# A two-layer kernel on one core: the quantised branch of the mixing layer is laid out by channels from tile 8 on

## The reference, cut to what matters

```
xn = layernorm(x)
x  = x + ssm_block(xn) + quantised_linear(xn)

quantised_linear(xn):
    for every token and every block of 32 channels:
        scale = max(max|xn| / 7.5, 1e-30)
        q     = xn / scale, each rounded to the nearest number of the FP6 (E2M3) grid
    out = (q * scale) @ wd.T + bias          # wd: the weight, quantised in the same way
```

## Time and profile before

| what | value |
|---|---|
| time, median of 3 runs | 2079.48 us (2079.25 to 2079.97) |
| time of the profiled execution | 2080.59 us |
| its span, first to last instruction | 2078.8 us |
| PE busy | 2063.7 us (99%) |
| DVE busy | 1523.1 us (73%) |
| ACT busy | 1095.0 us (53%) |
| POOL busy | 840.9 us (40%) |
| granted clock of PE | 0.999 of full speed |
| read from HBM, written to HBM | 160.88 MB, 100.79 MB |

### The profile page before, as it was taken

The page is one execution under the profiler, slowest core; times in us unless marked ns, Lnnn a source line. Parts: engine busy times, 40 slices in busy tenths (PEclk is TensorE's granted clock), DMA queues, the critical chain, the costliest instruction groups (busy, mean ns, idle before and its releaser), DMA issues.

```text
span 2078.8 us, 27463 instructions
## 1 busy us (share of the span) xinstructions
PE 2063.7 (99%) x9263; PEld 1645.9 (79%) x9263; DVE 1523.1 (73%) x2973; ACT 1095.0 (53%) x1842; POOL 840.9 (40%) x842
## 2 busy tenths in 40 slices
PE   9999999999999999999999999999999999999998
PEld 7887888444688888888888888788888888888887
DVE  6998775666787777776777875677777676677776
ACT  4555556223455555555555555755555555555553
POOL 1011110455545454554444453144444444444444
PEclk9999999999999999999999999999999999999999
DMA  5666662976533333333333332422222222222211
GB/s 199 251 220 226 202 210 103 292 254 208 176 122 102 108 116 103 131 102 102 122 119 105 115 119 101 152 71 72 71 72 74 90 91 86 88 71 72 71 41 41
DMA packets 179750, 263.47 MB, mean 127 GB/s; under 512 B 20377, under 2 KB 110745, under 8 KB 177050
## 3 DMA queue, kind: packets, MB, share of 16 engines
q1 hardware_dynamic: 166488, 238.18, 34.7%
q10 hardware_dynamic: 13122, 23.53, 3.1%
HBM read 160.88 MB, written 100.79 MB: 126 GB/s over the span
## 4 chain that ended last, share of the span: by engine, by line
PE 89%; DVE 5%; ACT 2%; issue 2%; POOL 1%; DMA 1%; SPq 0%; POOLq 0%; ACTq 0%
PE bank L102 23%; PE bank L104 23%; PE bank L103 23%; PE bank L1512 7%; PE bank L2068 3%; PE bank L901 3%; PE bank L922 3%; PE bank L919 3%; PE bank L1468 2%; PE bank L645 1%; DVE e_w_lo L1895 0%; DVE d_x L1364 0%; DVE d_xq L1335 0%; DVE d_stats L1366 0%; PE bank L1526 0%
## 5 line engine op out<-in xcount | busy, mean ns | idle before, releaser
L102 PE MATMUL bank<-e_ring,e_w_hi 128*128 128x512 f32 x512 | 200.8, 392 | 0.0
L103 PE MATMUL bank<-e_ring,e_w_hi 128*128 128x512 f32 x512 | 199.3, 389 | 0.0
L104 PE MATMUL bank<-e_ring,e_w_lo 128*128 128x512 f32 x512 | 199.3, 389 | 0.0
L1512 PE MATMUL bank<-d_kh,d_nat 128*128 128x512 f32 x768 | 191.1, 398 | 0.0
L1788 POOL TENSOR_TENSOR e_x<-e_x,e_beta 128x512 f32<-128x512 f32 x64 | 91.5, 1449 | 220.7 <-ACT e_y L1831 220.7
L1133 POOL TENSOR_TENSOR rstd<-d_var_eps,neg_half 128x1 f32<-128x1 f32 x64 | 35.7, 558 | 340.7 <-DVE d_var_eps L1375 340.7
L1842 ACT ACTIVATE e_kr<-bank 128x512 f32<-128x512 f32 x64 | 38.0, 594 | 247.6 <-PE bank L104 247.6
L1512 PEld LDWEIGHTS bank<-d_kh,d_nat 128*128 128x128 f32 x768 | 139.7, 188 | 26.9
L1913 DVE TENSOR_TENSOR e_ring<-e_mixed,e_ring 128x512 fp32r<-128x512 f32 x128 | 93.5, 731 | 88.0 <-ACT e_ring L1806 87.9
L1770 POOL TENSOR_TENSOR e_x<-e_x,e_ff 128x512 f32<-128x512 f32 x64 | 83.4, 1304 | 174.9 <-DVE e_ff L1979 174.9
L1380 DVE TENSOR_TENSOR d_nat<-d_xn,d_nat 128x512 fp32r<-128x512 f32 x64 | 86.0, 1345 | 78.1 <-ACT d_nat L1240 78.1
(11 more groups left out here) (226 smaller groups left out, 6300.0 us busy)
## 6 DMA issues: line engine op xcount, KB each, us to landing
scr_v<-b_vt SPq DMA_DIRECT2D x64, 256.0 KB, 2.7
scr_z<-b_zt SPq DMA_DIRECT2D x64, 256.0 KB, 2.1
c_z<-scr_z SPq DMA_DIRECT2D x64, 256.0 KB, 4.3
scr_y<-c_y ACTq DMA_DIRECT2D x64, 256.0 KB, 4.0
d_x<-in_L_attn_x SPq DMA_DIRECT2D x64, 256.0 KB, 3.6
d_v<-scr_v SPq DMA_DIRECT2D x32, 512.0 KB, 5.2
scr_x<-d_x SPq DMA_DIRECT2D x64, 256.0 KB, 2.3
scr_xnt<-d_xt SPq DMA_DIRECT2D x32, 512.0 KB, 4.1
```

What stands on the lines that cost most here:

```text
L102: eng.matmul(out, lhs[hi], rhs[hi], start=first, stop=False, skip_group_check=onto)
L103: eng.matmul(out, lhs[hi], rhs[lo], start=False, stop=False, skip_group_check=onto)
L104: return eng.matmul(out, lhs[lo], rhs[hi], start=False, stop=last, skip_group_check=onto)
L1512: mm = pe.matmul(BG[c][:, :], s[:, i, cols], r[:, j, :], start=M % NTB == 0 and i == j, stop=M % NTB == NTB - 1 and i == 1, skip_group_che ...
```

## The change

For tiles N of 8 and more (`BY_ROWS = 8`; group 2 of `project` begins there) the quantised branch is laid out with channels on the partitions:

1. `project` stores each normalised group 2 to 15 (1 MB) to HBM (`store_normalised`), on SP's queue, ahead of the loads of the next groups.
2. A copy of the tile's tokens is loaded (`load_tokens`) and normalised by ACT five turns ahead (`normalise_tokens`, in the place of `normalise_input`). At the end of DVE's turn N, `scale_tile(N+5)` takes the blocks' maxima, scales and reciprocals, and turns the 32 columns in squares of 32 by 32. There are two places for turned scales.
3. SP stores the turned scales (`store_scales`) and loads them back as rows that lie across 32 partitions each (`load_channels` for the reciprocals, with the tile of normalised x; `load_scales` for the scales, two places).
4. DVE's `row_step`s of tile N+2 are four instead of seven: multiply by the row of reciprocals, exponent bits, rounding constant, add. POOL subtracts, and multiplies by the row of scales instead of a broadcast column.
5. There is no `turn_q`. `high_q` (ACT) and `low_q` (DVE) read the SBUF tile `d_xq` where they read the PSUM bank.
6. Tokens for `sums` are loaded two turns ahead into two buffers; semaphores are merged, and some tiles get other places (`d_gt0`, `d_xa`, `d_inv_row`, `e_beta`).

```diff
+        def store_normalised(g):
+            if g > TURNED_GROUPS:
+                sp.wait_ge(xn_stored, 16 * (g - TURNED_GROUPS))
+            sp.wait_ge(xn_done, 2 * KT * g)
+            sp.dma_start(scr["xn"][g], xc[g % 2][:, :, :]).then_inc(xn_stored, 16)
...
+    def store_scales(N):
+        sp.wait_ge(s_step, SCALE_STEPS * (N - BY_ROWS + 1))
+        sp.dma_start(scr["scales"][N].rearrange("c (s i) -> s c i", s=P // QBLOCK), scales_turned[N % 2])\
+          .then_inc(s_stored, 16)
...
+    def load_channels(N):
+        b, m, h = tile_at(N)
+        sp.wait_ge(s_stored, 16 * (N - BY_ROWS + 1))
+        sp.wait_ge(prep, prep_done(N - 1, 1 if N > BY_ROWS else 0))
+        sp.wait_ge(q_lo, N - 2)
+        sp.dma_start(inv_row[:, :], row_of(N, 0)).then_inc(inv_in, 16)
+        cols = (m % 2 * 2 + h) * P
+        sp.dma_start(xq[N % 3][:, :].rearrange("p (k t) -> p k t", k=KT),
+                     scr["xn"][b * sh.NGB + m // 2][:, :, cols:cols + P]).then_inc(inv_in, 16)
+
+    def load_scales(N):
+        sp.wait_ge(q_done, N - 1)
...
+        sp.dma_start(scale_row[N % 2][:, :], row_of(N, 1)).then_inc(scale_in[N % 2], 16)
...
         for N in range(NT + 1):
+            if BY_ROWS <= N + 6 < NT:
+                load_tokens(N + 6)
+            if BY_ROWS <= N + 3 < NT:
+                load_channels(N + 3)
+                load_scales(N + 3)
+            if BY_ROWS <= N + 4 < NT:
+                store_scales(N + 4)
...
     def finish_quantising(N):
...
+        if N >= BY_ROWS:
+            pool.wait_ge(scale_in[N % 2], SCALES_FROM[N % 2] + 16 * ((N - BY_ROWS) // 2 + 1))
+            nc.gpsimd.tensor_tensor(tile[:, :], tile[:, :], scale_row[N % 2][:, :],
+                                    ALU.mult).then_inc(q_done, 1)
+            return
...
     def high_q(N):
-        act.wait_ge(q_full, N + 1)
-        nc.scalar.activation(qt[N % 2][:, 0, :, :], BB[:, :].rearrange("p (k t) -> p k t", k=KT), ACT.Copy)\
-          .then_inc(q_hi, 1)
+        if N < BY_ROWS:
+            act.wait_ge(q_full, N + 1)
+        else:
+            act.wait_ge(q_done, N + 1)
+            act.wait_ge(x2_full, N - 1)
+        nc.scalar.activation(qt[N % 2][:, 0, :, :], quantised(N), ACT.Copy).then_inc(q_hi, 1)
...
     def low_q(N):
         dve.wait_ge(q_hi, N + 1)
         tile = qt[N % 2]
-        nc.vector.tensor_tensor(tile[:, 1, :, :], BB[:, :].rearrange("p (k t) -> p k t", k=KT),
-                                tile[:, 0, :, :].bitcast(F32), ALU.subtract).then_inc(q_lo, 1)
+        nc.vector.tensor_tensor(tile[:, 1, :, :], quantised(N), tile[:, 0, :, :].bitcast(F32), ALU.subtract)\
+          .then_inc(q_lo, 1)
...
+    def scale_tile(N):
+        n = SCALE_STEPS * (N - BY_ROWS)
+        dve.wait_ge(xa_done, N - BY_ROWS + 1)
+        nc.vector.tensor_reduce(a_max, xa[N % 2][:, :].rearrange("p (b e) -> p b e", e=QBLOCK), AX.X, ALU.max,
+                                apply_absolute_value=True).then_inc(s_step, 1)
+        dve.wait_ge(s_step, n + 1)
+        nc.vector.tensor_scalar(scales[:, NBL:2 * NBL].rearrange("p (s k) -> p k s", k=KT),
+                                a_max.rearrange("p (k s) -> p k s", k=KT), 1.0 / FP6_MAX, SCALE_EPS,
+                                ALU.mult, ALU.max).then_inc(s_step, 1)
+        dve.wait_ge(s_step, n + 2)
+        nc.vector.reciprocal(scales[:, 0:NBL], scales[:, NBL:2 * NBL]).then_inc(s_step, 1)
+        dve.wait_ge(s_step, n + 3)
+        if N >= BY_ROWS + 2:
+            dve.wait_ge(s_stored, 16 * (N - BY_ROWS - 1))
+        nc.vector.transpose(scales_turned[N % 2], scales).then_inc(s_step, 1)
+
+    def row_step(N, k):
+        tile, p = xq[N % 3], N % 2
+        if k == 0:
+            dve.wait_ge(inv_in, 32 * (N - BY_ROWS + 1))
+            dve.wait_ge(q_done, N - 1)
+            ins_ = nc.vector.tensor_tensor(tile[:, :], tile[:, :], inv_row[:, :],
+                                           ALU.mult)
+        else:
+            dve.wait_ge(prep, prep_done(N, k))
+            ins_ = round_step(tile, magic[:, p, :], k - 1)
+        ins_.then_inc(prep, 1)
...
             low_keys(N - 3)
-            if N + 2 < NT:
+            if N + 2 < BY_ROWS:
                 for k in range(PREP):
                     prepare_step(N + 2, k)
+            elif N + 2 < NT:
+                for k in range(ROW_STEPS):
+                    row_step(N + 2, k)
...
             low_nat(N)
+            if BY_ROWS <= N + 5 < NT:
+                scale_tile(N + 5)
...
-            if N + 1 < NT:
+            if N + 1 < BY_ROWS:
                 turn_q(N + 1)
             outer(N - 3)
             keys(N - 2)
```

More of the change, by code:

```diff
@@ L171, in phase_project @@
         "v": [(v_stored[h], 16 * KT * NG // 2) for h in range(2)],
-        "sides": (right_done, KT * NG), "powers": (pow_step, 10),
+        "sides": (right_done, KT * NG), "powers": (pow_step, 10), "state_step": a_step, "third_in": (x2_in, 32),
     }
@@ L689, in phase_scan @@
     y_stored = [sem(f"c_y_stored{i}") for i in range(Y)]
-    zeroed = sem("c_zeroed")
+    zeroed, STEPS_BEFORE = project["state_step"], 19
     tab_done = sem("c_tab_done")
@@ L721, in load_first_z @@
         nc.sync.wait_ge(*project["split"])
+        nc.sync.wait_ge(*project["xn_stored"])
         nc.sync.wait_ge(*project["x1"])
@@ L952, in phase_mix @@
     xt = [front(f"d_xt{i}", [P, KT, 2 * P]) for i in range(2)]
-    gt = front("d_gt", [P, KT, D])
+    gt = [nc.alloc_sbuf_tensor_at("d_gt0", [P, KT, D], F32, offset=areas["tables"].begin["e_w_hi0"]),
+          front("d_gt", [P, KT, D])]
+    at = areas["tables"].begin["d_gt"]
+    xa = [nc.alloc_sbuf_tensor_at(f"d_xa{i}", [P, D], F32, offset=at + 4 * D * i) for i in range(2)]
+    inv_row = nc.alloc_sbuf_tensor_at("d_inv_row", [P, D], F32, offset=at + 4 * D * 2)
     u_pair = [areas["second_weight"].split_tile(f"d_ut{i}", [P, KT, 2 * P]) for i in range(2)]
@@ L973, in phase_mix @@
     ones = rest("d_ones", [P, 1])
-    const_in, sums_set, bias_done = keep["rows_in"], sem("d_sums_set"), sem("d_bias_done")
+    scale_area = rest("d_scales", [P, D])
+    scales, a_max = scale_area[:, 0:QBLOCK], scale_area[:, P:P + NBL]
+    scales_turned = [scale_area[:, (2 + i) * P:(2 + i) * P + QBLOCK] for i in range(2)]
+    const_in, sums_set = keep["rows_in"], sem("d_sums_set")
     x_ld = keep["x_ld"]
@@ L981, in phase_mix @@
     prep, q_sub, q_done = sem("d_prep"), sem("d_q_sub"), sem("d_q_done")
-    shift_set, xq_done = sem("d_shift_set"), sem("d_xq_done")
+    shift_set, SHIFT_AT, xq_done = keep["project"]["state_step"], 22, sem("d_xq_done")
     bank_open, x2_set, k_set = sem("d_bank_open"), sem("d_x2_set"), sem("d_k_set")
+    xa_ld = [sem(f"d_xa_ld{i}") for i in range(2)]
+    xa_done, s_step, s_stored = sem("d_xa_done"), sem("d_s_step"), sem("d_s_stored")
+    inv_in, scale_in = sem("d_inv_in"), [keep["project"]["third_in"][0], sem("d_scale_in")]
+    SCALES_FROM = [keep["project"]["third_in"][1], 0]
     gated, u_hi, u_lo = sem("d_gated"), sem("d_u_hi"), sem("d_u_lo")
@@ L1317, in shift_input, with round_step @@
                                        ALU.mult, ALU.mult).then_inc(shift_set, 1)
+    def scale_tile(N):
[10 more added lines that the diff above has]
+        dve.wait_ge(s_step, n + 3)
+        if N >= BY_ROWS + 2:
+            dve.wait_ge(s_stored, 16 * (N - BY_ROWS - 1))
[11 more added lines that the diff above has]
+        ins_.then_inc(prep, 1)
+    def round_step(tile, step, k):
+        if k == 0:
+            return nc.vector.tensor_scalar(step.bitcast(U32), tile[:, :].bitcast(U32), EXPONENT_BITS, None,
+                                           ALU.bitwise_and)
+        if k == 1:
+            return nc.vector.tensor_scalar(step, step, 1.0, ROUND_MAGIC, ALU.max, ALU.mult)
+        return nc.vector.tensor_tensor(tile[:, :], tile[:, :], step, ALU.add)
     def prepare_step(N, k):
@@ L1517, in sums_row @@
             pe.wait_ge(kacc_done, (b + 1) * NTB)
-            pe.matmul(BA[0:1, :], ones[:, :], kacc[b][:, :], start=True, stop=True).then_inc(ks_full, 1)
+            pe.matmul(BA[0:1, :], ones[:, :], kacc[b][:, :], start=True, stop=True).then_inc(end_full, 1)
         def values(b):
-            pe.wait_ge(ks_done, b + 1)
+            pe.wait_ge(kv_done, TAKEN * b + 1)
             pe.wait_ge(g_done, KT * (b + 1))
@@ L1664, in phase_second_layer @@
     gamma = over("d_bk", "e_gamma", [P, D])
-    beta = areas["rest"].tile("e_beta", [P, D])
+    beta = over("d_scales", "e_beta", [P, D])
     den = small("e_den", [P, 2, 2, HP])
```

123 lines of the change are left out of this document (78 added, 45 removed).

## The result

The changed kernel takes 2085.01 us (median of 10 runs, 2083.73 to 2087.06) against 2079.65 (2079.13 to 2080.49) for the kernel before in the same rounds: ratio 1.0026, 95% interval 1.0018 to 1.0034. It is 5.4 us slower, just over the 4.2 us that I took as the bound of "no change". The profiled execution took 2085.84 us with a span of 2084.0, 5.2 above that of before. The granted clock is 0.998.

The account below looks back on a forecast made before the run. PE was taken to bound the kernel. Terms +2.2 + 2.0 - 1.8 - 1.8 = +0.6 us on the profiled 2080.59, less 1.1, gave 2080 us beside a median of 2079.48; range 2057 to 2098.

Parts of the forecast that it names:

- Pace from PE to DVE and POOL: Steady mixing turns: the loop of DVE and POOL, 23.67 us per pair, replaces PE (22.71) as the pace.
- shared door: DVE instructions with two SBUF inputs, or SBUF-to-SBUF scale steps, wait for POOL's instruction under way, and the other way round.
- PE's 24.4 us: Tiles 8 to 63: each removed `turn_q` frees 0.43 to 0.44 us of PE, 24.4 over 56 tiles.
- The wait for `low_u`: PE's wait for POOL's `low_u`: covered by PE's other work; uncovered 0.2 us per pair while PE paces.
- Steady pairs, +2.2: Turns 8 to 58 without 34 to 37: 24 pairs, each 0.09 us longer, +2.2 us.
- Start of the new layout, +2.0: Turns 3 to 5, seven `prepare_step`s and a `scale_tile` on DVE: between 0 and 4 us, taken as +2.0.
- Finishing a batch, -1.8: Turns 34 to 37: PE has more to do and paces them, 4 x 0.44 = -1.8 us.
- The end, -1.8: Turns 59 to 62 have no `scale_tile` and PE paces again: 4 x 0.44 = -1.8 us.
- PE keeps the pace: Rival for the steady pairs: PE still paces, pair 22.7 to 22.9 us, total 2059 us; chance 0.17.
- `scale_tile` is not held: Rival: DVE and POOL pace, but POOL does not hold the scale step; pair 23.3, total 2071 us; chance 0.22.
- One more clash: Rival: in even turns a later `add_keys` holds DVE's row multiply, up to 1.29 us; total 2096 us; chance 0.22.
- Rows come late: Rival: DVE waits for loaded rows before its row multiply, 0.5 us per turn; about 2103 us; chance 0.05.

Follow-up runs that it names:

- the best kernel: The changed kernel with POOL's `low_u` ahead of root and shift and DVE's scale steps ahead of `low_nat`: 2053.96 us, ratio to before 0.9875.
- the run with both moves: The changed kernel with POOL's addition held back to `bn_stats` and DVE's scale steps ahead of `low_nat`: 2063.11 us.

## Why the prediction was right or wrong

*Pace from PE to DVE and POOL: right.* (The rows that it was counted from, are those of the turn from 618.44 us, ahead of the steady stretch; the steady odd turn before takes 13.02 us, not 12.49, with DVE waiting in it.) The pair is 23.59, predicted 23.67. Counted from `sums` at 740.81, the addition ends at 10.26 (predicted 10.27), the mask step at 10.56 (10.56), and the next `sums` starts at 12.80 (12.8); the even turn took 10.79 (10.87). The shared door held as used: `low_q` delays the shift (0.60 us long), the multiply takes 1.29, the scale step is held to 0.57. PE waits 0.6 us a pair for `low_u` (predicted "near 1").

*PE's 24.4 us: right as work, never all to be had.* Without transposes the old layout gives 17 us, and with transposes put back the new one loses 2.6. At 22.73 the best kernel confirms PE's 22.71. So of 24.4 us some 7 never came in the old layout, and DVE's longer row took the other 17 and 5 us more. The wait for `low_u`, which I had called covered, costs 0.3 us a pair where PE is the pace (the run with both moves).

*Steady pairs, +2.2: right in kind, too large.* The pair came out 0.01 us above the old one, not 0.09. Turns 9 to 33 gave +0.40, 41 to 49 +0.07, 1.7 us less together than I had counted.

*Start of the new layout, +2.0: the term that was mis-sized.* Turns 3 to 9 gave +5.9 (turns 1 to 3: +0.3). I had bounded it by 0 and 4, with DVE's added work at 1.4 us a turn and some slack under it. It cost 2.00 us in turn 4 and 1.99 in turn 5; turns 6 to 8 add 0.9 and turn 9 adds 1.0. The reason for turns 4 and 5 is in two numbers. The scale step is held there by POOL's addition (578.87 to 580.16):

```profile
578.34 0.69 DVE L1423 TENSOR_REDUCE d_scales<-d_xa 128x16 f32<-128x512 f32 x1
579.06 1.13 DVE L1426 TENSOR_SCALAR d_scales<-d_scales 128x16 f32<-128x16 f32 x1
580.23 0.25 DVE L1430 RECIPROCAL d_scales<-d_scales 128x16 f32<-128x16 f32 x1
580.51 0.21 DVE L1434 STREAM_TRANSPOSE d_scales<-d_scales 128x32 f32<-128x32 f32 x1
580.65 0.65 DVE L1488 SCALAR_TENSOR_TENSOR d_kh<-bank,d_kh 128x512 fp32r<-128x512 f32 x1
```

From 578.34 to 580.65 are 2.31 us, not 1.4. And DVE had hardly any slack there: in the same turn before, its row from `low_nat` to `sums` has one gap:

```profile
579.65 0.69 DVE L1355 SCALAR_TENSOR_TENSOR d_kh<-bank,d_kh 128x512 fp32r<-128x512 f32 x1 [0.30 <-ACT d_kh L1216]
```

2.31 - 0.30 = 2.01, what the turn lost. The run with the scale steps ahead of `low_nat` has turns 4 and 5 as long as before, to 0.01 us. Turn 9 is 11.37 us long, where turns 11, 13 and so on take 10.79. In the turn ahead of it PE had stood for `low_u`, three times as long as in a steady pair:

```profile
627.42 0.47 PE L102 MATMUL bank<-d_w,d_ut 128*128 128x512 f32 x1 [1.91 <-POOL d_ut L1205]
```

and in turn 9 `low_q` comes 0.26 us later behind `sums` (0.17 of it a wait for ACT) and the scale step takes 0.80 us instead of 0.56. That the one caused the other is not shown by a run.

*Finishing a batch, -1.8: right.* Turns 33 to 41 gave -1.95, and with the transposes put back only -0.2: PE does pace them.

*The weights, a term I did not have.* Turns 49 to 57 gave +3.1. I had counted those turns as steady ones. The splits cost the kernel before 0.9 us over turns 51 to 60, against steady pairs of 23.58; with DVE as the pace, each stands in its row. Moving them took 4.0 us out of these turns, of which the medians show 1.9 at the end.

*The end, -1.8:* turns 57 to 63 gave -1.2.

The sum is +6.6 from turn 1 on and -1.35 of scatter ahead of it: +5.3. I had +0.6. The 1.7 us too many on the steady pairs and the scatter hid part of the 7 us too few on start and weights: that the forecast missed by only 5 us is in that part luck. The direction came out in the class to which I gave 0.29; the class that I thought likeliest (faster, 0.38) did not occur. The time is inside the range, 5 us above the forecast. Of the rivals, "PE keeps the pace" and "`scale_tile` is not held" are refuted by the rows above. "One more clash" did not occur: in the even turn the addition ends at 737.49, and the row product starts at 738.56 and takes its free 0.68. "Rows come late" did not either; no wait for a row is listed in the steady stretch, though a tile of `d_x` now lands in 7.0 us where it took 3.6.

## What to carry to other kernels

When an edit relieves the bounding engine, work out which engine paces next, and then go through every stretch where that engine has extra duties (start, weights, end): what was hidden there is hidden no longer. Then look for its waits, not for its work: DVE stood 1.68 us a turn in front of one subtraction with 1.8 us of independent work right behind it, and exchanging the two was worth more than the whole change had cost. Before moving work on an engine that excludes another, write down what it will stand beside: the same move of `low_u` gave 13 us in one kernel and cost 13 in the other.

## What the runs showed of the hardware

DVE instructions with two SBUF inputs, and scale and mask steps from SBUF to SBUF, gave way to a POOL instruction under way, and POOL to them (its subtraction took 1.74 us behind `low_nat` and 1.29 free): a DVE mask step of 0.43 us took 1.40 beside the addition and 2.52 beside `low_u`; the scale step on 16 numbers took 0.18 free, 0.56 to 0.57 in the loop, 1.13 at the start beside the addition and 1.72 beside `low_u`. Not held were `bn_stats`, which takes 0.69 us beside the addition (736.60 and 736.64 in the run with the addition moved) and 0.69 beside `low_u` (730.38, in the best kernel), and `sums`, whose one input lies in PSUM: 0.69 there (729.66). The Trainium skill has this ("SBUF — State Buffer", Who interferes with whom): the one that issues second blocks until the first has finished; the traces agree, with the numbers here. That the length shown for a tiny instruction is mostly waiting was easy to overlook: 26 of these scale steps are 14.9 us of DVE's "busy" time in the steady stretch, where 26 free ones would be 4.7. Nor is PE's busy share a proof that it is the pace: PE showed 299.21 of 300 us busy in the run with both moves, while each pair lost 0.3 us to waits too short to be listed.
